# A gated two-branch feed-forward on one core: the median search counts two of its four rows in one packed sum, and all its rounds stand in the second gate/up stage

## The chip, the cores and the metric

The kernel runs on one core of a Trainium2 chip. The metric is the device time of one execution in microseconds (us), the median of several runs. The engines are named as in the profile: PE is TensorE's matmul, PEld its weight load, DVE is VectorE, ACT is ScalarE, POOL is GpSimd, SP is SyncE, which issues every transfer.

## The reference

For 2048 tokens of 1024 features, with an inner width I = 2752:

```
xn = layernorm(x)                               # 2048 x 1024
s  = silu(xn @ w_gate.T)                        # 2048 x 2752
     in each token: the 1376 entries of smallest |s| are set to 0 (ties by index)
s  = (s * (xn @ w_up.T)) @ w_down.T             # branch A
g  = silu((silu(xn @ W_gate.T) * (xn @ W_up.T)) @ W_down.T)   # branch B
out = x + s * g
```

All is in fp32. The kernel keeps that precision by splitting each operand in a high and a low part and making three matmuls for each product (high x high, high x low, low x high).

## The kernel before

The tokens go in four blocks (b = 0 to 3) of 512, four tiles of 128 tokens each. PE goes through four stages in each block:

- **Stage A**: gate and up of branch A. Its results become `keys` (|silu(gate)|, four rows of 2752 fp32 in each partition, one for each token tile) and `prods`.
- **Stage B**, the second gate/up stage: 22 chunks of 128 inner features of branch B (21 whole ones and a half), 48 matmuls of 512 columns for a whole chunk (L875 to L877). After chunk c ACT makes its silu (`silu_b`, L1077), and DVE multiplies it by up (`product_b`, L1554), which frees the chunk's two PSUM banks for chunk c + 4.
- **Stage BD**: the down projection of branch B (L632), from `hid_ring`, which ACT and DVE fill chunk by chunk (`hid_split` and `hid_lo_part`, L1397). Beside it DVE ends the search, corrects ties (`mask_ties`, `mask_prods`) and turns the masked products for branch A (`turn_first`, L1622), whose last transpose releases ACT for `split_turned` and then for the silu of branch B's output (L1136), which PE waits for.
- **Stage AD**: the down projection of branch A (L632 again).

The search for each token's median key needs keys alone. It finds the 31 bits of a float in 31 rounds: a round counts in each of the four rows how many keys lie below a candidate, accepts the bit or not, and posts the next candidate (`cand_ready`). DVE counts rows 0 and 1 (L1380, one instruction a row, a comparison whose results are summed by the accumulator), ACT counts rows 2 and 3 at the same time (`count`, L961). The small instructions behind them (L1384 accept, L1386 bit, L1387 found, L1389 next candidate) are DVE's. Rounds 0 to 29 stand in stage B: two ahead of the first chunk's product, then one or two behind the product of each of the first 20 chunks (`ROUNDS_AFTER`, `TWO_AFTER`). Round 30 stands in stage BD, behind the first four low parts.

In block 0 the weights come raw. ACT makes each tile's high part (`hi`, L928), POOL its low part (`low`, L1206, a subtraction of two tensors in SBUF with 1024 columns; 512 for stage B's last two tiles), and SP writes both to DRAM for the later blocks. In the later blocks stage B's tiles are loaded ready-made, and POOL does nothing in it. In block 0 POOL's low part of each of stage B's tiles 4 to 43 waits until a certain round begins:

```python
c, odd = divmod(m - B0 - 4, 2)
pool.wait_ge(cand_ready, ROUNDS_AFTER[c].start + (odd if c not in BOTH_HIGHS else 0) + 1)
```

A chunk of stage B uses two tiles, the ring holds four, and PE waits for the low part of each tile of block 0.

Of the kernel before, what the change touches and what calls it, by code (L numbers as in the profile page):

```python
# [10 lines left out]
ALU = mybir.AluOpType  # L11
# [5 lines left out]
I = 2752  # L17
K_ZERO = int(0.5 * I)
# [10 lines left out]
NJ = -(-I // P)  # L29
# [44 lines left out]

ROUNDS = 31
DVE_ROWS = 2
ACT_ROWS = NT - DVE_ROWS
PAIRS = 4
GROUPS = NJ // PAIRS
ROUNDS_FIRST = 2  # L80
TWO_AFTER = (1, 4, 6, 9, 11, 14, 16, 19)

ROUNDS_AFTER = []
for chunk in range(PAIRS * GROUPS):
    first = ROUNDS_AFTER[-1].stop if chunk else ROUNDS_FIRST
    ROUNDS_AFTER.append(range(first, first + (2 if chunk in TWO_AFTER else 1)))
ROUNDS_B = ROUNDS_AFTER[-1].stop
# [2 lines left out]
assert all(len(ROUNDS_AFTER[c]) == 1 for c in BOTH_HIGHS)  # L90


LOWS_ROUND = 5
LOWS_CHECK = 7
LOWS_MASKS = ((8, 9, 10, 10, 11, 11), (12, 14, 14, 14, 15, 15), (17, 18, 18, 19, 19, 20), (21, 22, 22, 22, 22, 22))

# [48 lines left out]
assert all(chunk_of(n % 2, n // 4, n // 2 % 2) == K_ORDER[n] for n in range(KC))  # L145
assert TILES % RING == 0 and B0 % RING == 0 and BD0 % RING == 0 and AD0 % RING == 2
assert 2 * TAIL == P and NJ == PAIRS * GROUPS + 2 and NJ == 4 * LOOP4 + 6
assert ROUNDS_B + 1 == ROUNDS and LOWS_MASKS[-1][-1] == NJ

assert AD0 % RING == RING - 2  # L150
assert TURN_FIRST - AHEAD >= -(-16 * NT // SQUARES_STEP)
# [38 lines left out]
def done(b, m):  # L190

    return b * BLOCK + m + 1 + RING
# [55 lines left out]
def build(nc, x, w_a, w_rest, w_b, w_tail, wd_b, wd_a, out):  # L248
# [8 lines left out]
    with ExitStack() as ctx:  # L257
        place = [base]

        def at(name, words_shape, dt, offset):  # L260
            return nc.alloc_sbuf_tensor_at(name, [P, *words_shape], dt, offset=offset)

        def take(nbytes):
            got = place[0]
            place[0] += -(-nbytes // 32) * 32
            assert place[0] <= nc.sbuf_usable_end, place[0]
            return got

        def sem(name):
            return ctx.enter_context(nc.semaphore(name))  # L270
# [6 lines left out]
        keys = key_buf[:, 0:NT * I].rearrange("p (t i) -> p t i", t=NT)  # L277
# [25 lines left out]
        ranks = at("ranks", [I], I16, ranks_at)  # L303
# [15 lines left out]
        def small(name, shape, dt=F32):  # L319
            n = 4  # L320
            for s in shape:
                n *= s
            return at(name, shape, dt, take(n))
# [14 lines left out]
        counts = small("counts", [NT])  # L338
        limits = small("limits", [NT])
        sign_sum = small("sign_sum", [NT])  # L340
        need2 = small("need2", [1])
        found_f = found[:, :].bitcast(F32)
        cand_f = cand[:, :].bitcast(F32)

# [52 lines left out]
        sel_step = sem("sel_step")  # L397
# [524 lines left out]
        def _(act):  # L922
            def hi(b, m):

                if m < TILES and is_split(b, m):
                    q, w = m % RING, width(m)
                    act.wait_ge(landed[q], m // RING * 16 + 16)
                    act.activation(w_hi[q][:, 0:w], w_raw[q][:, 0:w], ACT.Copy).then_inc(hi_ready, 1)  # L928
# [19 lines left out]
            def run(b, first_block):  # L948
                def hid_split(dst, src, rows=P):
                    if rows == TAIL:  # L950

                        act.activation(hid_ring[TAIL:P, dst, 1, :], src[0:TAIL], ACT.Copy)
                    act.activation(hid_ring[0:rows, dst, 0, :], src[0:rows], ACT.Copy).then_inc(hid_hi, 1)  # L953

                def count(n):

                    act.wait_ge(cand_ready, b * (ROUNDS + 1) + n + 1)
                    for t in range(DVE_ROWS, NT):
                        if t > DVE_ROWS:
                            act.wait_ge(act_counted, b * (ROUNDS * ACT_ROWS) + n * ACT_ROWS + (t - DVE_ROWS))  # L960
                        act.activation(signs_row[:, :], keys[:, t, :], ACT.Sign, bias=cand_f[:, t:t + 1], scale=-1.0,  # L961
                                       accum_out=counts[:, t:t + 1]).then_inc(act_counted, 1)
# [141 lines left out]
                def signs_of(t):  # L1104
                    if t < DVE_ROWS:
                        act.wait_ge(cand_ready, b * (ROUNDS + 1) + (ROUNDS + 1))
                    else:
                        act.wait_ge(found_ready, b + 1)

                    act.wait_ge(signs_used, b * NT + (2 if t == NT - 1 else 1))  # L1110
                    act.activation(signs[t], keys[:, t, :], ACT.Sign, bias=found_f[:, t:t + 1], scale=-1.0,
                                   accum_out=sign_sum[:, t:t + 1]).then_inc(signed, 1)

                for j in range(NJ):
                    if j + AHEAD < NJ:
                        if j > 0:
                            act.wait_ge(tiles_done, done(b, BD0 + j - 1))
                        if j == 0:
                            act.wait_ge(b_free, b * NJ + (NJ + PAIRS))
                        hid_split((j + AHEAD) % RING, hid_b[:, j + AHEAD, :], P if j + AHEAD < NJ - 1 else TAIL)  # L1120
                        if j + AHEAD >= STAGED:
                            hi(b, BD0 + j + AHEAD)
                    if j == 0:
                        count(ROUNDS_B)
                    for t in range(NT):
                        if j == SIGNS_AT[t]:
                            signs_of(t)
# [50 lines left out]
            for b in range(NB):  # L1178
                run(b, b == 0)
# [84 lines left out]
        def _(dve):  # L1264
            dve.memset(need2[:, :], 0.0).then_inc(consts, 1)
            dve.memset(ones[:, :], 1)
            dve.memset(eps[:, :], EPS)
            dve.memset(limits[:, 0:DVE_ROWS], K_ZERO - 0.5)
            dve.memset(limits[:, DVE_ROWS:NT], 2 * K_ZERO - I - 0.5).then_inc(consts, 1)
            dve.sem_inc(a_free, NT)  # L1270
            dve.sem_inc(b_free, PAIRS)
# [64 lines left out]
                dve.tensor_tensor(xnT[:, k, 1, tokens], ps[:, X_BANK + i, 0:STAGE * P], xnT[:, k, 0, tokens].bitcast(F32),  # L1336
                                  ALU.subtract).then_inc(xn_ready, 1)

            ROUND_STEPS = DVE_ROWS + 3
            CHECK_STEPS = ACT_ROWS + 2  # L1340

            def xn_low(b, n):
# [28 lines left out]
                    dve.tensor_tensor(lo, raw, high.bitcast(F32), ALU.subtract).then_inc(w_low, 1)  # L1371

            def run(b, last_block):
                def search_round(n):
                    dve.wait_ge(cand_ready, b * (ROUNDS + 1) + n + 1)
                    done = b * (ROUNDS * ROUND_STEPS) + n * ROUND_STEPS
                    for t in range(DVE_ROWS):
                        if t > 0:
                            dve.wait_ge(sel_step, done + t)
                        dve.tensor_scalar(ranks[:, :], keys[:, t, :], cand_f[:, t:t + 1], 0.0, ALU.is_lt, ALU.add,  # L1380
                                          accum_out=counts[:, t:t + 1]).then_inc(sel_step, 1)
                    dve.wait_ge(sel_step, done + DVE_ROWS)
                    dve.wait_ge(act_counted, b * (ROUNDS * ACT_ROWS) + n * ACT_ROWS + ACT_ROWS)
                    dve.tensor_tensor(accept[:, :], counts[:, :], limits[:, :], ALU.is_le).then_inc(sel_step, 1)  # L1384
                    dve.wait_ge(sel_step, done + (DVE_ROWS + 1))
                    dve.tensor_scalar(bit[:, :], bit[:, :], 1, None, ALU.logical_shift_right).then_inc(sel_step, 1)  # L1386
                    dve.copy_predicated(found[:, :], accept[:, :], cand[:, :]).then_inc(sel_step, 1)  # L1387
                    dve.wait_ge(sel_step, done + ROUND_STEPS)
                    dve.tensor_tensor(cand[:, :], found[:, :], bit[:, :], ALU.bitwise_or).then_inc(cand_ready, 1)  # L1389
# [156 lines left out]
                def product_b(c):  # L1546
                    pair = c % PAIRS
                    dve.wait_ge(b_silu, b * NJ + (c + 1))
                    dve.wait_ge(tiles_done, done(b, B0 + 2 * c + 1))
                    chunk = hid_b[:, c, :]  # L1550
                    if c == NJ - 1:
                        dve.tensor_tensor(chunk[0:TAIL], ps[TAIL:P, 2 * pair, :], chunk[0:TAIL], ALU.mult).then_inc(b_free, 1)
                    else:
                        dve.tensor_tensor(chunk, ps[:, 2 * pair + 1, :], chunk, ALU.mult).then_inc(b_free, 1)  # L1554

                for n in range(ROUNDS_FIRST):
                    search_round(n)
                for c, rounds in enumerate(ROUNDS_AFTER):
                    product_b(c)
                    for n in rounds:  # L1560
                        search_round(n)
                product_b(NJ - 2)

                dve.wait_ge(b_free, b * NJ + (NJ - 1 + PAIRS))
# [46 lines left out]
                def lows_to(n):  # L1611
                    for j in range(lows[0], n):
                        hid_lo_part(j % RING, hid_b[:, j, :], b * (2 * NJ) + j, j == NJ - 1)
                    lows[0] = n
# [15 lines left out]
                    return dve.transpose(dst, src)  # L1630

                lows_to(AHEAD + 1)
                search_round(ROUNDS_B)
                lows_to(LOWS_ROUND)
                dve.wait_ge(cand_ready, b * (ROUNDS + 1) + (ROUNDS + 1))
                dve.memset(accept[:, :], 0)
                check_found()
# [92 lines left out]
            for b in range(NB):  # L1730
                run(b, b == NB - 1)

            t = NT - 1
# [47 lines left out]
```

## Time and profile before

| what | value |
|---|---|
| median of 3 runs (lowest to highest) | 2782.26 us (2779.91 to 2783.34) |
| the profiled execution's own time | 2784.59 us |
| its span in the profile | 2782.8 us |
| PE busy | 2753.9 us, 99% of the span |
| DVE busy | 2307.4 us, 83% |
| ACT busy | 1352.7 us, 49% |
| POOL busy | 388.3 us, 14% |
| DMA | 614.28 MB, 221 GB/s |

The kernel's time is PE's matmuls and the few places where PE stands still. A faster DVE or ACT shortens it only where PE waits for them. A slower one lengthens it as soon as the reserve between the engines is used up.

### The profile page before, as it was taken

How to read it: one execution, taken by the hardware profiler on the slowest of the kernel's cores; microseconds unless marked ns; L12 is line 12 of the kernel's file. 1: busy time of each engine (PE TensorE's matmuls, PEld its weight loads, DVE VectorE, ACT ScalarE, POOL GpSimd, SP SyncE). 2: the span in 40 equal slices, each digit the busy share in tenths (PEclk: the TensorE clock that was granted, in tenths of full speed). 3: DMA queues.
4: the chain of work that ended last, by engine and by line, in shares of the span. 5: the costliest groups of instructions: out<-in, count | busy, mean ns of one | idle time of the engine just before them, and what ended most of it. 6: DMA issues, size and time to landing. Idle time of an engine off the chain costs nothing. (4 is left out here: it accounts for less than half of the span.)

```text
span 2782.8 us, 31374 instructions
## 1 busy us (share of the span) xinstructions
PE 2753.9 (99%) x12204; PEld 2281.1 (82%) x12204; DVE 2307.4 (83%) x3002; ACT 1352.7 (49%) x1386; POOL 388.3 (14%) x161
## 2 busy tenths in 40 slices
PE   9999999999999999999999999999999999999999
PEld 7778888878788888888878888888887888888887
DVE  7676999999967698998986678999897767999971
ACT  4234998332444477631144557671115446776110
POOL 5565443044400000000020000000011000000000
PEclk9999999999999999999999999999999999999999
DMA  6898888579766555556656655555666664555564
GB/s 235 308 328 286 293 288 280 211 251 357 255 193 196 181 188 192 189 203 219 249 190 195 192 180 190 195 196 194 240 223 195 193 196 173 195 196 193 189 233 170
DMA packets 135097, 614.28 MB, mean 221 GB/s; under 512 B 12752, under 2 KB 12752, under 8 KB 89168
## 3 DMA queue, kind: packets, MB, share of 16 engines
q1 hardware_dynamic: 134992, 612.94, 63.2%
q8 instruction: 58, 0.95, 0.1%
q14 instruction: 47, 0.39, 0.0%
HBM read 492.31 MB, written 120.59 MB: 220 GB/s over the span
## 5 line engine op out<-in xcount | busy, mean ns | idle before, releaser
L632 PE MATMUL ps<-w_split,hid_ring 128*128 128x512 f32 x4096 | 935.2, 390 | 6.8 <-ACT hid_buf L1136 4.6
L632 PEld LDWEIGHTS ps<-w_split,hid_ring 128*128 128x128 f32 x4096 | 769.4, 188 | 171.5 <-issue 7.9
L1380 DVE TENSOR_SCALAR_CACHE_REDUCE ranks<-key_buf,cand 128x2752 int16<-128x2752 f32 x248 | 762.9, 3076 | 5.8
L961 ACT ACTIVATE signs_row<-key_buf,cand 128x2752 bf16<-128x2752 f32 x248 | 642.6, 2591 | 191.6 <-DVE cand L1389 182.0
L877 PE MATMUL ps<-xnT,w_split 128*128 128x512 f32 x1376 | 535.3, 389 | 0.0
L876 PE MATMUL ps<-xnT,w_split 128*128 128x512 f32 x1376 | 535.3, 389 | 0.0
L875 PE MATMUL ps<-xnT,w_split 128*128 128x512 f32 x1376 | 535.3, 389 | 0.0
L1206 POOL TENSOR_TENSOR w_split<-w_raw,w_split 128x1024 fp32r<-128x1024 f32 (+2 forms) x118 | 290.2, 2467 | 377.3 <-ACT w_split L928 137.0
L875 PEld LDWEIGHTS ps<-xnT,w_split 128*128 128x128 f32 x1376 | 258.3, 188 | 53.7
L876 PEld LDWEIGHTS ps<-xnT,w_split 128*128 128x128 f32 x1376 | 258.3, 188 | 53.6
L877 PEld LDWEIGHTS ps<-xnT,w_split 128*128 128x128 f32 x1376 | 258.3, 188 | 53.3
L928 ACT ACTIVATE w_split<-w_raw 128x1024 fp32r<-128x1024 f32 (+2 forms) x118 | 122.8, 1043 | 252.5 <-DMA w_raw<-w_a 125.9
L847 PE MATMUL ps<-w_split,s_split 128*128 128x512 f32 x936 | 217.0, 389 | 0.0
L938 ACT ACTIVATE w_split<-w_raw 128x1024 fp32r<-128x1024 f32 x144 | 151.1, 1050 | 133.7 <-DMA w_raw<-t_dram 76.9
L1371 DVE TENSOR_TENSOR w_split<-w_raw,w_split 128x1024 fp32r<-128x1024 f32 x144 | 172.0, 1210 | 47.1 <-ACT w_split L938 46.8
L847 PEld LDWEIGHTS ps<-w_split,s_split 128*128 128x128 f32 x936 | 175.7, 188 | 36.4
L1227 POOL TENSOR_TENSOR prods<-prods 128x1024 f32<-128x1024 f32 x3 | 8.7, 2906 | 1297.3 <-DVE prods L1354 1297.3
L953 ACT ACTIVATE hid_ring<-key_buf 128x512 fp32r<-128x512 f32 x88 | 54.3, 630 | 268.3 <-PE ps L632 191.3
L847 PE MATMUL ps<-w_split,xnT 128*128 128x512 f32 x720 | 167.6, 390 | 0.0
L953 ACT ACTIVATE hid_ring<-hid_buf 128x512 fp32r<-128x512 f32 x88 | 55.1, 631 | 226.8 <-PE ps L632 225.1
L847 PEld LDWEIGHTS ps<-w_split,xnT 128*128 128x128 f32 x720 | 135.6, 188 | 28.3
L782 PE MATMUL ps<-w_split,xnT 128*128 128x512 f32 (+1 forms) x368 | 140.5, 382 | 5.8 <-POOL w_split L1206 3.4
(146 smaller groups left out, 2907.0 us busy)
## 6 DMA issues: line engine op xcount, KB each, us to landing
w_split<-split SPq DMA_DIRECT2D x272, 1024.0 KB, 4.8
split<-w_split SPq DMA_DIRECT2D x72, 1024.0 KB, 6.8
w_raw<-w_a SPq DMA_DIRECT2D x100, 512.0 KB, 4.2
w_raw<-t_dram SPq DMA_DIRECT2D x78, 512.0 KB, 3.3
w_raw<-w_b SPq DMA_DIRECT2D x42, 512.0 KB, 4.9
w_extra_raw<-t_dram SPq DMA_DIRECT2D x42, 512.0 KB, 3.6
t_dram<-t_buf SPq DMA_DIRECT2D x20, 1024.0 KB, 8.6
w_extra_raw<-w_a SPq DMA_DIRECT2D x30, 512.0 KB, 3.6
```

Of the source, the lines that this page charges most:

```text
L632: ins = pe.matmul(ps[:, 2 * t + half, :], h, w[:, half * TB:(half + 1) * TB], start=(first and n == 0), stop=last and stop)
L782: pe.matmul(ps[:, bank, 0:wide], hi, w_high[:, cols], start=first, stop=False)
L847: ins = pe.matmul(ps[:, W_BANK[p] + t, :], tokens_of(p, pair, n, part, t), w[:, cols], start=(p in (P4, P1, P6, P5) and pair == 0 and n == ...
L875: pe.matmul(ps[:, bank, :], hi, xnT[:, k, 0, :], start=(first and n == 0), stop=False)
L876: pe.matmul(ps[:, bank, :], hi, xnT[:, k, 1, :], start=False, stop=False)
L877: ins = pe.matmul(ps[:, bank, :], lo, xnT[:, k, 0, :], start=False, stop=(last and k == KC - 1))
L928: act.activation(w_hi[q][:, 0:w], w_raw[q][:, 0:w], ACT.Copy).then_inc(hi_ready, 1)
L938: act.activation(high, raw, ACT.Copy).then_inc(hi_ready, 1)
L961: act.activation(signs_row[:, :], keys[:, t, :], ACT.Sign, bias=cand_f[:, t:t + 1], scale=-1.0, accum_out=counts[:, t:t + 1]).then_inc(act ...
L1206: pool.tensor_tensor(w_lo[q][:, 0:w], w_raw[q][:, 0:w], w_hi[q][:, 0:w].bitcast(F32), ALU.subtract).then_inc(lo_ready, 1)
L1371: dve.tensor_tensor(lo, raw, high.bitcast(F32), ALU.subtract).then_inc(w_low, 1)
L1380: dve.tensor_scalar(ranks[:, :], keys[:, t, :], cand_f[:, t:t + 1], 0.0, ALU.is_lt, ALU.add, accum_out=counts[:, t:t + 1]).then_inc(sel_st ...
```

## The change

DVE's two counts become one packed sum. The first instruction compares row 0 with its candidate and writes 4096 for each key below it (no sum). The second compares row 1 (0 or 1 for each key at or above its candidate), adds the first one's result and sums: 4096 x (count of row 0) + (count of row 1). Two instructions of one column take the sum apart by rounding. The limits of rows 0 and 1 change to fit. A chunk's `product_b` moves from ahead of its first round into that round, behind DVE's counts and ahead of the wait for ACT's. `TWO_AFTER` has nine chunks where it had eight, so all 31 rounds stand in stage B, and stage BD has none. `LOWS_ROUND`, which ordered the low parts around the old round 30, is gone. POOL's waits are unchanged in form and follow the new `ROUNDS_AFTER`.

```diff
+PACK = 4096.0
+PACK_ROUND = 1.5 * 2.0 ** 23 * PACK
-TWO_AFTER = (1, 4, 6, 9, 11, 14, 16, 19)
+TWO_AFTER = (1, 3, 6, 8, 10, 12, 14, 16, 18)
-LOWS_ROUND = 5
@@ ACT, stage BD
-                    if j == 0:
-                        count(ROUNDS_B)
@@ DVE
-            dve.memset(limits[:, 0:DVE_ROWS], K_ZERO - 0.5)
+            dve.memset(limits[:, 0:1], PACK * K_ZERO - 0.5)
+            dve.memset(limits[:, 1:2], K_ZERO - I - 0.5)
@@ a round
-                    for t in range(DVE_ROWS):
-                        if t > 0:
-                            dve.wait_ge(sel_step, done + t)
-                        dve.tensor_scalar(ranks[:, :], keys[:, t, :], cand_f[:, t:t + 1], 0.0, ALU.is_lt, ALU.add,
-                                          accum_out=counts[:, t:t + 1]).then_inc(sel_step, 1)
-                    dve.wait_ge(sel_step, done + DVE_ROWS)
+                    dve.tensor_scalar(ranks[:, :], keys[:, 0, :], cand_f[:, 0:1], PACK, ALU.is_lt, ALU.mult).then_inc(sel_step, 1)
+                    dve.wait_ge(sel_step, done + 1)
+                    dve.scalar_tensor_tensor(out=ranks[:, :], in0=keys[:, 1, :], scalar=cand_f[:, 1:2], in1=ranks[:, :],
+                                             op0=ALU.is_ge, op1=ALU.add, accum_out=counts[:, 0:1]).then_inc(sel_step, 1)
+                    dve.wait_ge(sel_step, done + 2)
+                    dve.tensor_scalar(above[:, :], counts[:, 0:1], float(-(I // 2)), PACK_ROUND, ALU.add, ALU.add).then_inc(sel_step, 1)
+                    dve.wait_ge(sel_step, done + 3)
+                    dve.scalar_tensor_tensor(out=counts[:, 1:2], in0=above[:, :], scalar=PACK_ROUND, in1=counts[:, 0:1],
+                                             op0=ALU.subtract, op1=ALU.subtract).then_inc(sel_step, 1)
+                    if product is not None:
+                        product_b(product)
+                    dve.wait_ge(sel_step, done + 4)
                     dve.wait_ge(act_counted, b * (ROUNDS * ACT_ROWS) + n * ACT_ROWS + ACT_ROWS)
                     dve.tensor_tensor(accept[:, :], counts[:, :], limits[:, :], ALU.is_le).then_inc(sel_step, 1)
@@ stage B
                 for c, rounds in enumerate(ROUNDS_AFTER):
-                    product_b(c)
                     for n in rounds:
-                        search_round(n)
+                        search_round(n, c if n == rounds.start else None)
@@ stage BD
                 lows_to(AHEAD + 1)
-                search_round(ROUNDS_B)
-                lows_to(LOWS_ROUND)
```

## Rows read from the trace of the kernel before

**Rows 1.** Page, part 1: busy time, share of the span, instructions.
```profile
PE 2753.9 (99%) x12204; PEld 2281.1 (82%) x12204; DVE 2307.4 (83%) x3002; ACT 1352.7 (49%) x1386; POOL 388.3 (14%) x161
```
**Rows 2.** PE's waits, whole span: us in total, times, longest.
```profile
PE ps L847 <- DVE xnT L1345: 5.0, 3, 2.1
PE ps L632 <- ACT hid_buf L1136: 4.6, 1, 4.6
```
**Rows 3.** Line L632's matmuls: ns min/median/max, first and last start (us).
```profile
L632 PE MATMUL ps<-w_split,hid_ring x4096: 387/389/764, 489.5 to 2777.8; 128*128 128x512 f32 x196
```
**Rows 4.** Windows, stage B of blocks 0, 1: PE, PEld, DVE, ACT, POOL, clock, DMA.
```profile
256.00:490.00 234.00, 234.00 (x1034) 193.81 (x1033) 218.33 (x272) 211.53 (x187) 98.72 (x42) 1.00 0.84 286
960.00:1181.00 221.00, 221.00 (x977) 183.06 (x976) 203.98 (x253) 164.28 (x137) 0.00 (x0) 1.00 0.53 190
```
**Rows 5.** DVE's timeline, block 0: first count, a round, a product (start, us).
```profile
257.49 3.08 DVE L1380 TENSOR_SCALAR_CACHE_REDUCE ranks<-key_buf,cand 128x2752 int16<-128x2752 f32 x1
...
480.28 0.16 DVE L1384 TENSOR_TENSOR accept<-counts,limits 128x4 uint32<-128x4 f32 x1
...
480.95 3.08 DVE L1380 TENSOR_SCALAR_CACHE_REDUCE ranks<-key_buf,cand 128x2752 int16<-128x2752 f32 x1
...
484.07 3.08 DVE L1380 TENSOR_SCALAR_CACHE_REDUCE ranks<-key_buf,cand 128x2752 int16<-128x2752 f32 x1
...
487.19 0.17 DVE L1384 TENSOR_TENSOR accept<-counts,limits 128x4 uint32<-128x4 f32 x1
...
487.67 0.16 DVE L1389 TENSOR_TENSOR cand<-found,bit 128x4 uint32<-128x4 uint32 x1
487.75 0.69 DVE L1554 TENSOR_TENSOR hid_buf<-ps,hid_buf 128x512 f32<-128x512 f32 x1
```
**Rows 6.** ACT's timeline in the same round.
```profile
480.95 2.59 ACT L961 ACTIVATE signs_row<-key_buf,cand 128x2752 bf16<-128x2752 f32 x1 [3.68 <-DVE cand L1389]
...
486.16 0.19 ACT L961 ACTIVATION_READ_ACCUMULATOR signs_row<-key_buf,cand 128x1 f32 x1
```
**Rows 7.** Groups by line and shape: busy us, mean ns; idle before.
```profile
L1459 DVE TENSOR_SCALAR key_buf<-key_buf 128x512 uint32<-128x512 uint32 x60 | 22.8, 424 | 0.0
L1602 DVE TENSOR_SCALAR ranks<-ranks,need 128x2752 int16<-128x2752 int16 x16 | 15.0, 936 | 0.6
L1590 DVE TENSOR_SCALAR ranks<-signs_row 128x2752 int16<-128x2752 bf16 x8 | 7.0, 870 | 0.0
L1418 DVE TENSOR_SCALAR key_buf<-key_buf 128x192 uint32<-128x192 uint32 x16 | 3.1, 255 | 0.1
```
**Rows 8.** Groups by line: two-input and scan instructions of 2752 columns.
```profile
L1592 DVE TENSOR_TENSOR_SCAN ranks<-ranks 128x2752 int16<-128x2752 int16 x16 | 94.3, 5892 | 0.6
L1607 DVE TENSOR_TENSOR prods<-prods,ranks 128x2752 f32<-128x2752 f32 x16 | 48.4, 3026 | 2.3
```
**Rows 9.** Line L1380, all 248 counts: ns min/median/max.
```profile
L1380 DVE TENSOR_SCALAR_CACHE_REDUCE ranks<-key_buf,cand x248: 3069/3079/3081, 257.5 to 2549.2; 128x2752 int16<-128x2752 f32 x124
```
**Rows 10.** Timelines of POOL and DVE at two places of block 0.
```profile
264.01 2.42 POOL L1206 TENSOR_TENSOR w_split<-w_raw,w_split 128x1024 fp32r<-128x1024 f32 x1 [4.48 <-ACT w_split L928]
...
264.20 2.24 DVE L1389 TENSOR_TENSOR cand<-found,bit 128x4 uint32<-128x4 uint32 x1
...
587.27 5.89 DVE L1592 TENSOR_TENSOR_SCAN ranks<-ranks 128x2752 int16<-128x2752 int16 x1
...
589.10 6.25 POOL L1206 TENSOR_TENSOR w_split<-w_raw,w_split 128x1024 fp32r<-128x1024 f32 x1 [3.20 <-ACT w_split L928]
...
593.07 2.83 DVE L1397 TENSOR_TENSOR hid_ring<-hid_buf,hid_ring 128x512 fp32r<-128x512 f32 x1
```
**Rows 11.** Waits of POOL for candidates, whole span.
```profile
POOL w_split L1206 <- DVE cand L1389: 113.9, 26, 7.2
```
**Rows 12.** Windows, PE alone, behind its 4.6 us wait: busy, clock, DMA.
```profile
613.00:621.00 8.00, 8.00 (x25) 0.70 0.50 193
```

More of the change, by code:

```diff
@@ L76 @@
 DVE_ROWS = 2
+PACK = 4096.0
+PACK_ROUND = 1.5 * 2.0 ** 23 * PACK
+assert I < PACK and I // 2 < PACK / 2 and PACK * (I + 1) < 2 ** 24
 ACT_ROWS = NT - DVE_ROWS
@@ L147 @@
 assert 2 * TAIL == P and NJ == PAIRS * GROUPS + 2 and NJ == 4 * LOOP4 + 6
-assert ROUNDS_B + 1 == ROUNDS and LOWS_MASKS[-1][-1] == NJ
+assert ROUNDS_B == ROUNDS and LOWS_MASKS[-1][-1] == NJ
 assert AD0 % RING == RING - 2
@@ L341, in build @@
         need2 = small("need2", [1])
+        above = small("above", [1])
         found_f = found[:, :].bitcast(F32)
@@ L1337, in x_low @@
                                   ALU.subtract).then_inc(xn_ready, 1)
-            ROUND_STEPS = DVE_ROWS + 3
+            ROUND_STEPS = DVE_ROWS + 5
             CHECK_STEPS = ACT_ROWS + 2
@@ L1373, in run, with search_round @@
             def run(b, last_block):
-                def search_round(n):
+                def search_round(n, product=None):
                     dve.wait_ge(cand_ready, b * (ROUNDS + 1) + n + 1)
                     done = b * (ROUNDS * ROUND_STEPS) + n * ROUND_STEPS
-                    for t in range(DVE_ROWS):
-                        if t > 0:
-                            dve.wait_ge(sel_step, done + t)
-                        dve.tensor_scalar(ranks[:, :], keys[:, t, :], cand_f[:, t:t + 1], 0.0, ALU.is_lt, ALU.add,
-                                          accum_out=counts[:, t:t + 1]).then_inc(sel_step, 1)
-                    dve.wait_ge(sel_step, done + DVE_ROWS)
+                    dve.tensor_scalar(ranks[:, :], keys[:, 0, :], cand_f[:, 0:1], PACK, ALU.is_lt, ALU.mult).then_inc(sel_step, 1)
[10 more added lines that the diff above has]
+                    dve.wait_ge(sel_step, done + 4)
                     dve.wait_ge(act_counted, b * (ROUNDS * ACT_ROWS) + n * ACT_ROWS + ACT_ROWS)
                     dve.tensor_tensor(accept[:, :], counts[:, :], limits[:, :], ALU.is_le).then_inc(sel_step, 1)
-                    dve.wait_ge(sel_step, done + (DVE_ROWS + 1))
+                    dve.wait_ge(sel_step, done + (DVE_ROWS + 3))
                     dve.tensor_scalar(bit[:, :], bit[:, :], 1, None, ALU.logical_shift_right).then_inc(sel_step, 1)
```

## The prediction

> **What bounds the kernel now.** I read the page's busy times first. PE is busy for 99% of the span, DVE for 83%, ACT for half, POOL for 14% [rows 1]. So the time can fall only by what PE stands still, some 29 us in all (2782.8 - 2753.9), and it can rise wherever another engine falls behind PE. Next come PE's waits. Most are a microsecond or two at block borders. One alone is large: 4.6 us for ACT's silu of branch B's output [rows 2]. It stands in block 0, between stages BD and AD. Then the windows of stage B, where the rounds are: PE is busy for all of them, in block 0 as in block 1 [rows 4]. The reader is to see in the same rows that DVE is nearly full there (218 of 234 us, 204 of 221), and that block 0 alone has POOL at work beside it: 42 instructions, 98.7 us.
>
> PE cannot get faster in stage B. All the change can win is the 4.6 us in stage BD, and what it can lose is DVE's reserve in stage B.
>
> **A round, before and after.** Before, count to count on DVE takes 3.12 us (480.95 to 484.07, the accumulator's read included), the second count as much (to 487.19), and accept to next count 0.67 us (480.28 to 480.95): 6.91 us [rows 5]. ACT's two counts take 5.4 us (480.95 to 486.35) [rows 6], so DVE sets the pace.
>
> The first new instruction (compare, times 4096) has no sum. Its nearest rows are one-input instructions without a sum: 4-byte ones take 424 ns at 512 columns and 255 at 192 [rows 7], 0.53 ns for each column more, while the count with a sum takes 3079 ns for 2752 [rows 9], 1.1 each. I take the half rate: 424 + 2240 x 0.53 = 1.61 us, plus 0.07 for the candidate read per partition (936 against 870 ns for two int16 instructions with and without such an operand [rows 7]), so 1.68, and 1.71 with the 0.03 gap. Its upper end is the old count without its read, 3.0 us. The second one reads two tensors in SBUF (keys fp32, ranks int16) and sums. The two-input row with just these kinds takes 3026 ns without a sum [rows 8], the summed one-input row 3079. I take 3.12 to the next start. Its upper end is the scan, which runs at half that pace (5892 ns [rows 8]). The two one-column instructions cost 0.20 us each, like the small ones of the tail (487.67 back to 487.19 has such steps). Sum: 1.71 + 3.12 + 0.40 + 0.67 = 5.90 us, and a product inside a round adds 0.65 (0.69 busy [rows 5]).
>
> Where POOL is still (blocks 1 to 3) ACT is about level: 5.4 + 0.1 + 0.67 = 6.2 us for a round. 31 rounds and 20 products take at most 31 x 6.2 + 20 x 0.65 = 205 us. The old order had 230 us for 30 (257.49 to 487.83). So three blocks get slack in stage B. Round 30 leaves stage BD, 6.9 us less for DVE there, but PE waits for nothing in the BD stages of blocks 1 to 3, so these gain nothing. ACT loses its 5.4 us of counting in stage BD too. No transfer is added or moved.
>
> **Block 0: POOL against DVE.** This decides. Look at the two places of [rows 10]. At 264.01 a low part starts on POOL; DVE's candidate instruction of 4 columns with two SBUF inputs starts at 264.20 and takes 2.24 us instead of 0.16: it ends when POOL does. At 589.10 a low part starts under DVE's scan and takes 6.25 us instead of 2.4: it waits for the scan's end (593.1), and then DVE's next two-input instruction at 593.07 takes 2.83 us instead of 0.69, because POOL slipped in between. So the two take turns, each for a whole instruction. The old counts stand outside this: 248 of them lie between 3069 and 3081 ns [rows 9], though POOL's low parts run beside them, started with them by the wait for `cand_ready` [rows 11]. The old order puts each low part under an instruction that does not mind it. The Trainium skill has this rule in "SBUF — State Buffer", Who interferes with whom: one-input instructions with an accumulator output stay clear of the port pair shared with GpSimd, the 2-port modes and two-input ones contend for it, and the pair is held for the whole instruction. By that rule both new instructions contend; the trace agrees for the two-input kind.
>
> In the new kernel POOL's low part is released at the same moment as before, when a round begins. DVE's compare starts in the same moment (before, a count starts 0.2 us behind the candidate). If POOL comes first, the compare waits; if second, POOL slips in behind the compare and the sum waits. Either way DVE loses what the rows show: 2.24 - 0.16 = 2.08, or 2.83 - 0.69 = 2.14, say 2.1 us for each low part. The 20 chunks have 40 low parts with such a gate, 38 of 1024 columns and 2 of 512, and two more stand at the stage's start: 40 x 2.1 + 2 x 1.0 = 86 us. Where two low parts fall in one round (behind a chunk with a single round), the second waits for the sum and then holds up the small two-input instruction behind it, at the same price. ACT's reserve hides nothing, since a round of 8.0 us is above ACT's 6.2.
>
> Stage B of block 0 on DVE: 31 x 5.90 = 183, 20 x 0.65 = 13, and 86, together 282 us. From 257.5 the last candidate is at 539.5. Stage B's last tile's low part waits for that candidate (its gate is round 31's), so 1.3 us of POOL and the second half of the last chunk's matmuls (12 x 0.227 = 2.7 us; 234 us by 1034 [rows 4]) follow: stage BD begins at 543.5, not at 489.5 [rows 3]. That is **54 us** later. The reserve of the ring is included: it shifts where PE stalls, not the sum, since all rounds and products precede stage BD. With lags of this kind PE stops for some 3 us in each chunk; its granted clock then may fall to its lower level (after the 4.6 us stop the window shows 0.70 of 2.4 GHz [rows 12]), but a chunk at DVE's pace of 14 us (282 by 20; against 48 x 0.227 = 10.9) has room for that, so I add nothing.
>
> **The gain.** In stage BD of block 0 DVE is 6.9 us earlier, the last `turn_first` too, ACT's silu with it, and the 4.6 us wait goes, with the clock it cost: 8 us at 0.70 lose 8 x 0.30 = 2.4 us. That is 7.0 us. What is late next is the block border, at 1 to 2 us, unchanged.
>
> **Sum:** 2784.6 + 54 - 7 = 2831.6 for an execution like the profiled one, which lies 2.3 us above the median: **2829 us**.
>
> **The rivals.** 0.2% (5.6 us) is about what a measurement tells from no change.
>
> *No contention worth the name (ends faster).* One mechanism: DVE's sum does not need what POOL holds, because its second input is int16 or because POOL's wait behind the compare puts it beside something harmless. Then only the gain stands: 2782.3 - 7 = 2775. The stage has some 25 us of room (230 less 205), so it holds up to a price of 0.6 us for each of the 42 low parts. For it: no row shows this instruction beside POOL. Against: even 4 columns of a two-input instruction waited 2.1 us. Chance 0.08, and 0.04 for something in between that ends within 0.2%.
>
> *The sum runs at half rate.* Then it takes 5.9 us as the scan does, a round 8.7, and 31 rounds with products 283 us in every block, 53 more than before; block 0 has 86 more. 4 x 53 + 86 - 7 = +291: 3073 us. The Trainium skill warns of this in "Vector Engine (DVE) Microarchitecture Reference", Points that are easy to get wrong: scalar-tensor-tensor with two non-bf16 SBUF sources halves throughput, as no port is left for the accumulator's readback. No row here shows such an instruction wide; the two-input row without a sum runs whole. Chance 0.07.
>
> *The compare does not run at double rate*, so the packed count saves nothing. A round is 7.2 us (3.0 + 3.12 + 0.4 + 0.67), 31 rounds and products 236 us, 6 too many in each block. It would then also be clear of POOL, as the old count is, and only the second low part of a pair (some 10) meets the sum: 4 x 6 + 4 + 21 - 7 = +42, 2824 us. Against: the 4-byte rows at 0.53 ns a column. Chance 0.05.
>
> **Chances and range.** Contention at its price: 0.76, with 2810 to 2845 as its own range (a low part at 1.6 to 2.4 us, the compare up to 0.1 more, a few us of clock). Faster 0.08 + 0.01, within 0.2% 0.03, slower 0.88. The range 2795 to 2855 holds the likeliest but for its far ends, and the slow compare; it leaves out both the gain alone and the half rate.
>
> **What the profile would show.** Stage B of blocks 1 to 3: PE busy throughout, DVE well under 190 us of 221. Stage B of block 0: PE waits for L1206, some 50 us in total over many places; the wide sum at 3.1 us in blocks 1 to 3 and 5.2 in block 0; POOL's low parts over 2.4 us, 4 with the wait for the compare. The wait of 4.6 us for L1136 is gone. I am wrong if the sum's maximum is its median, if PE's waits in stage B of block 0 are nil, or if the wide sum takes near 6 us in all blocks.

## The result, and the profile after

The changed kernel takes 2835.12 us (median of 4 runs, 2833.63 to 2836.62), the kernel before 2782.26 us beside it: a ratio of 1.019, 95% interval 1.0177 to 1.0203. It is 53 us slower. Two executions of the kernel before, one here (4641.44 us) and one in a later sitting (4632.36 us), ran far slower than all its others and stand in no ratio. The forecast was 2829 us, slower, within 2795 to 2855. The profiled execution took 2834.48 us with a span of 2832.7 us.

PE's waits in the changed kernel (us in total, times, longest), answering to [rows 2]:

```profile
PE ps L879 <- POOL w_split L1208: 32.6, 18, 4.1
...
PE ps L636 <- ACT hid_buf L1138: 4.6, 1, 4.6
```

The first row is new: PE stands in stage B (L879 to L881 now) for POOL's low parts (L1208). The second was to vanish and did not. The windows of stage B, blocks 0 and 1 (PE, PEld, DVE, ACT, POOL, clock, DMA), answer to [rows 4], and PE alone to the stretches of block 0's stage:

```profile
256.00:545.00 289.00, 256.38 (x1044) 204.56 (x1043) 277.53 (x308) 216.65 (x191) 112.06 (x42) 0.95 0.68 239
...
1015.00:1235.00 220.00, 220.00 (x972) 182.19 (x971) 175.58 (x286) 166.56 (x141) 0.00 (x0) 1.00 0.54 191
```

```profile
400.00:500.00 100.00, 88.78 (x355) 0.93 0.67 236
```

In block 1 all is as hoped: PE full, DVE down from 204 to 176 us. In block 0 DVE is full for the whole stage (277.5 of 289) and PE is not. Only 33 us of the 50 that the stage grew by are idle PE. The other 18 are PE at work for longer: it is busy for 251.2 us from 256 to 539.8, where the stage took 233.5 before, with its clock at the lower level for some of the time (0.95 and 0.93 of 2.4 GHz). DVE sets the pace, so this is no extra loss but for the stage's last matmuls, and it makes the waits look smaller than they are. Line L636's matmuls tell where stage BD begins, 539.8 against 489.5 us [rows 3]:

```profile
L636 PE MATMUL ps<-w_split,hid_ring x4096: 387/389/763, 539.8 to 2827.8; 128*128 128x512 f32 x196
```

The two wide instructions and the small sum (groups by line: busy us, mean ns; then their ns min/median/max), answering to [rows 9]:

```profile
L1383 DVE SCALAR_TENSOR_TENSOR ranks<-key_buf,cand,ranks 128x2752 int16<-128x2752 f32 x124 | 402.6, 3247 | 4.4
...
L1381 DVE TENSOR_SCALAR ranks<-key_buf,cand 128x2752 int16<-128x2752 f32 x124 | 268.0, 2162 | 4.4
...
L1388 DVE SCALAR_TENSOR_TENSOR counts<-above,counts 128x1 f32<-128x1 f32 x124 | 23.6, 190 | 4.3
```

```profile
L1381 DVE TENSOR_SCALAR ranks<-key_buf,cand x124: 1652/1654/3909, 255.2 to 2573.6; 128x2752 int16<-128x2752 f32 x124
...
L1383 DVE SCALAR_TENSOR_TENSOR ranks<-key_buf,cand,ranks x124: 3083/3085/5111, 258.7 to 2575.3; 128x2752 int16<-128x2752 f32 x124
...
L1388 DVE SCALAR_TENSOR_TENSOR counts<-above,counts x124: 159/159/2095, 262.1 to 2578.6; 128x1 f32<-128x1 f32 x124
```

The medians are the bare prices: 1654, 3085, 159 ns. The means lie above them, by 0.51, 0.16 and 0.03 us. Times 124 that is 63 + 20 + 4 = 87 us of waiting. The old counts had a minimum and a maximum 12 ns apart. How the waiting looks in two rounds of block 0 (DVE's and POOL's timelines: start, us):

```profile
297.97 3.84 DVE L1381 TENSOR_SCALAR ranks<-key_buf,cand 128x2752 int16<-128x2752 f32 x1
301.84 5.11 DVE L1383 SCALAR_TENSOR_TENSOR ranks<-key_buf,cand,ranks 128x2752 int16<-128x2752 f32 x1
...
308.53 3.90 DVE L1381 TENSOR_SCALAR ranks<-key_buf,cand 128x2752 int16<-128x2752 f32 x1
312.46 3.08 DVE L1383 SCALAR_TENSOR_TENSOR ranks<-key_buf,cand,ranks 128x2752 int16<-128x2752 f32 x1
```

```profile
298.01 6.06 POOL L1208 TENSOR_TENSOR w_split<-w_raw,w_split 128x1024 fp32r<-128x1024 f32 x2 [5.71 <-DVE cand L1399]
308.57 2.40 POOL L1208 TENSOR_TENSOR w_split<-w_raw,w_split 128x1024 fp32r<-128x1024 f32 x1 [4.51 <-DVE cand L1399]
```

At 308.57 one low part runs its plain 2.40 us and the compare takes 3.90 in place of 1.65. At 298.01 two low parts follow each other: the first holds up the compare (2.2 us), the second waits for the compare and then holds up the sum (2.0 us).

### The profile page after: what moved, and what is told of

Its sections match the earlier page's. It is cut to its first block and busy times, and to the rows that moved or that the text cites. A ratio compares the mean times of both kernels' runs of the same rounds, so it can differ in the third digit from the quotient of the medians.

```text
span 2832.7 us, 31499 instructions
## 1 busy us (share of the span) xinstructions
PE 2770.5 (98%) x12204; PEld 2287.1 (81%) x12204; DVE 2251.1 (79%) x3127; ACT 1352.6 (48%) x1386; POOL 398.9 (14%) x161
## 5 line engine op out<-in xcount | busy, mean ns | idle before, releaser
L636 PE MATMUL ps<-w_split,hid_ring 128*128 128x512 f32 x4096 | 935.2, 390 | 7.4 <-ACT hid_buf L1138 4.6
L636 PEld LDWEIGHTS ps<-w_split,hid_ring 128*128 128x128 f32 x4096 | 769.3, 188 | 172.1 <-issue 7.9
L879 PE MATMUL ps<-xnT,w_split 128*128 128x512 f32 x1376 | 543.1, 395 | 32.6 <-POOL w_split L1208 32.6
L881 PE MATMUL ps<-xnT,w_split 128*128 128x512 f32 x1376 | 541.5, 394 | 0.0
L880 PE MATMUL ps<-xnT,w_split 128*128 128x512 f32 x1376 | 541.2, 393 | 0.0
L1383 DVE SCALAR_TENSOR_TENSOR ranks<-key_buf,cand,ranks 128x2752 int16<-128x2752 f32 x124 | 402.6, 3247 | 4.4
L1208 POOL TENSOR_TENSOR w_split<-w_raw,w_split 128x1024 fp32r<-128x1024 f32 (+2 forms) x118 | 300.2, 2551 | 416.8 <-DVE cand L1399 155.1
L879 PEld LDWEIGHTS ps<-xnT,w_split 128*128 128x128 f32 x1376 | 261.8, 190 | 95.0 <-POOL w_split L1208 40.4
L881 PEld LDWEIGHTS ps<-xnT,w_split 128*128 128x128 f32 x1376 | 261.6, 190 | 55.1
L880 PEld LDWEIGHTS ps<-xnT,w_split 128*128 128x128 f32 x1376 | 261.7, 190 | 54.5
L1381 DVE TENSOR_SCALAR ranks<-key_buf,cand 128x2752 int16<-128x2752 f32 x124 | 268.0, 2162 | 4.4
```

The costliest lines, as they stand in the source:

```text
L636: ins = pe.matmul(ps[:, 2 * t + half, :], h, w[:, half * TB:(half + 1) * TB], start=(first and n == 0), stop=last and stop)
L879: pe.matmul(ps[:, bank, :], hi, xnT[:, k, 0, :], start=(first and n == 0), stop=False)
L880: pe.matmul(ps[:, bank, :], hi, xnT[:, k, 1, :], start=False, stop=False)
L881: ins = pe.matmul(ps[:, bank, :], lo, xnT[:, k, 0, :], start=False, stop=(last and k == KC - 1))
L1208: pool.tensor_tensor(w_lo[q][:, 0:w], w_raw[q][:, 0:w], w_hi[q][:, 0:w].bitcast(F32), ALU.subtract).then_inc(lo_ready, 1)
L1381: dve.tensor_scalar(ranks[:, :], keys[:, 0, :], cand_f[:, 0:1], PACK, ALU.is_lt, ALU.mult).then_inc(sel_step, 1)
```

## The experiments

Theory 1 is the prediction's: DVE's new instructions and POOL's low parts take turns. Rival 2 is that the new order costs by itself. Each run's ratio is to the kernel before, with its 95% interval.

**POOL writes and does not read.** This is the changed kernel, but the low-part pass of block 0's stage B is left out of the result, for tiles 4 to 43.

```diff
+                if B0 + 4 <= m < BD0:
+                    pool.memset(w_lo[q][:, 0:w].bitcast(F32), 0.0).then_inc(lo_ready, 1)
+                    return
```

> The changed kernel, but in block 0's stage B the low parts of tiles 4 to 43 are not computed: POOL fills them with zero, at the same moments, and reads nothing (the low-part pass of branch B's gate and up in block 0 is left out of the result; all matmuls, waits and transfers stay). Theory 1 (DVE's new instructions and POOL's low parts take turns, 2.1 us for each of some 42): POOL's instruction gets shorter, near 1 us for a write of 1024 columns by the size of DVE's and ACT's one-tensor instructions, so at most half of the 86 us is left and the wide sum, which only shares the read side, is never longer than 3.1 us. Stage B has 25 us of room: 2783 to 2800 us. Rival 2 (the new order of rounds and of the gates stalls PE, whatever POOL reads): the time stays at 2835.

Measured: 2780.1 us, ratio 0.9993 (0.9983 to 1.0002). The whole loss is gone; the time is 3 us below the expected range, which had kept up to half of the waiting. Rival 2 falls, since order, waits and gates are unchanged in the program. The first two fences are DVE's and POOL's timelines, the third the range of the wide sum:

```profile
350.71 1.65 DVE L1384 TENSOR_SCALAR ranks<-key_buf,cand 128x2752 int16<-128x2752 f32 x1
352.40 3.08 DVE L1386 SCALAR_TENSOR_TENSOR ranks<-key_buf,cand,ranks 128x2752 int16<-128x2752 f32 x1
```

```profile
351.01 2.25 POOL L1209 MEMSET w_split<- 128x1024 f32 x1 [4.47 <-ACT w_split L932]
354.37 0.95 POOL L1209 MEMSET w_split<- 128x1024 f32 x1 [1.11 <-ACT w_split L932]
```

```profile
L1386 DVE SCALAR_TENSOR_TENSOR ranks<-key_buf,cand,ranks x124: 3083/3084/3087, 260.2 to 2524.1; 128x2752 int16<-128x2752 f32 x124
```

The write at 354.37 runs beside the wide sum in 0.95 us and leaves it at 3.08. The one at 351.01 comes 0.3 us behind a compare, and takes 2.25 us: it waits for the compare's end at 352.4, then runs. So the compare excludes even a write that comes behind it, and the sum only excludes an instruction of POOL that reads. The Trainium skill states both ("SBUF — State Buffer", Who interferes with whom); the trace agrees, with these numbers. This run changes more than the read, though. The write is shorter than the low part, and it starts at another moment: all but the last of these writes are released by ACT's high part, most of them 0.3 to 0.8 us behind a compare (351.01 against 350.71), and no longer together with the compare by the candidate. Whether a write that comes first would hold up the compare is not shown. That it is the sharing that costs rests on this run together with those below. The 4.6 us wait is still there in this run, although nothing delays stage B.

**Block 0 as before, blocks 1 to 3 as after.**

```diff
+PACKED = (False, True, True, True)      # by block
+ALL_IN_B = (False, True, True, True)    # 31 rounds in stage B, or 30
```

> Block 0 exactly as in the kernel before (two summed counts, 30 rounds in stage B, the 31st in stage BD), blocks 1 to 3 exactly as in the changed kernel. Theory 1: all of the loss is in block 0, where alone POOL computes in stage B, and blocks 1 to 3 neither lose nor gain: 2783 within 3 us. If the packed form costs something in every block (another cost of the new instructions, or of a lack of time in stage B), three quarters of the loss stay, some 2820. If the time freed in stage BD of blocks 1 to 3 were worth something, it would be below 2779.

Measured: 2782.77 us, ratio 1.0003 (0.9994 to 1.0013). All of the loss is in block 0, and the slack of blocks 1 to 3 is worth nothing that the interval (2 us less to 4 us more) could show. The compare's mean there is its plain price:

```profile
L1403 DVE TENSOR_SCALAR ranks<-key_buf,cand 128x2752 int16<-128x2752 f32 x93 | 153.8, 1653 | 3.3
```

**The move alone**: the changed kernel's order, with the old pair of counts in every round.

```diff
+PACKED = (False, False, False, False)
+ALL_IN_B = (True, True, True, True)
```

> The new order alone: 31 rounds in stage B in all blocks, the new chunks with two rounds, the product inside the round, POOL's gates as in the changed kernel, but each round counts its two rows with the old pair of summed instructions. Theory 1: no contention; 31 x 6.91 + 13 = 227 us on DVE against 230, and 1.3 + 2.7 us in block 0 behind the last candidate for the last tile's low part: 2783 to 2795. Rival 2 (the order is what costs): 2825 or more.

Measured: 2783.27 us, ratio 1.0001 (0.9991 to 1.001). 31 old rounds fit into stage B of every block, without packing; stage BD of block 0 begins at 489.6 us. The kernel never needed faster counts to make the move. And the move wins nothing. DVE's timeline in stage BD shows why:

```profile
499.17 0.68 DVE L1432 TENSOR_TENSOR hid_ring<-hid_buf,hid_ring 128x512 fp32r<-128x512 f32 x1
501.58 0.69 DVE L1432 TENSOR_TENSOR hid_ring<-hid_buf,hid_ring 128x512 fp32r<-128x512 f32 x1 [1.73 <-ACT hid_ring L968]
506.79 0.69 DVE L1432 TENSOR_TENSOR hid_ring<-hid_buf,hid_ring 128x512 fp32r<-128x512 f32 x1 [4.52 <-ACT hid_ring L968]
...
528.55 0.69 DVE L1432 TENSOR_TENSOR hid_ring<-hid_buf,hid_ring 128x512 fp32r<-128x512 f32 x1 [0.52 <-ACT hid_ring L968]
```

DVE waits three times for one of ACT's high parts: 1.73 + 4.52 + 0.52 = 6.8 us. That is the 6.9 us that round 30 left; the low part at 520.54 comes at 520.78 in the kernel before, so DVE is ahead no longer. What ACT waited for ahead of these high parts (its timeline):

```profile
500.93 0.61 ACT L968 ACTIVATE hid_ring<-hid_buf 128x512 fp32r<-128x512 f32 x1
506.12 0.63 ACT L968 ACTIVATE hid_ring<-hid_buf 128x512 fp32r<-128x512 f32 x1 [4.58 <-PE ps L647]
...
527.88 0.63 ACT L968 ACTIVATE hid_ring<-hid_buf 128x512 fp32r<-128x512 f32 x1 [2.23 <-PE ps L647]
```

The second and the third wait for PE to free a slot of `hid_ring`. The first shows no wait for PE: ACT came to it at once from its sums over the signs (L1126). PE's slots come 5.44 us apart here (506.12 to 511.56), so by my estimate that slot was free at 500.7, hardly earlier.

**The packing alone**: the old order, the new counts.

```diff
+PACKED = (True, True, True, True)
+ALL_IN_B = (False, False, False, False)   # and the product ahead of the round
```

> The packed count alone: old order (30 rounds in stage B, the 31st in stage BD, product ahead of the chunk's first round), each round with the new packed pair. Theory 1: 30 x 5.90 + 13 + 86 = 276 us in stage B of block 0, so stage BD begins near 535 and not at 489.5: +46 us, 2829 (2820 to 2840). Rival 2: 2783.

Measured: 2815.9 us, ratio 1.0113 (1.0096 to 1.013). The packing carries the loss, but 34 us of it (27 to 36 by the ratio's interval), not 46 as I expected: the value lies below the expected range. Stage BD begins at 522.0 us, 17.8 before the changed kernel's. Where a product stands ahead of a round (DVE, then POOL):

```profile
486.30 0.69 DVE L1590 TENSOR_TENSOR hid_buf<-ps,hid_buf 128x512 f32<-128x512 f32 x1
486.91 3.37 DVE L1404 TENSOR_SCALAR ranks<-key_buf,cand 128x2752 int16<-128x2752 f32 x1
```

```profile
486.46 2.37 POOL L1221 TENSOR_TENSOR w_split<-w_raw,w_split 128x1024 fp32r<-128x1024 f32 x1 [5.71 <-DVE cand L1425]
```

POOL starts under the product, which has one input in PSUM and takes its usual 0.69 us, so the compare waits 1.7 us and not 2.2. That gave theory 4, on the place of the product, tested last.

**The low parts on DVE.** All the work is done and nothing is shared: DVE computes the low parts of tiles 4 to 43 behind its counts.

```diff
+                    if b == 0:
+                        for m in LOWS_IN[n]:     # the tiles whose gate is this round
+                            dve_low(m)           # waits for hi_ready, one tensor_tensor
```

> The changed kernel, but in block 0's stage B DVE itself computes the low parts of tiles 4 to 43, one or two behind the counts of each round, and POOL is still. The work is all done; only the sharing is gone. Theory 1: each costs DVE its own 1.24 us (the 1210 ns of the later blocks' low parts and a gap) in place of 2.1 us of waiting: 257.5 + 183 + 13 + 50 = 503, so stage BD begins near 505 to 508, and the time is 2798 (2792 to 2806). A theory in which it is the mere number of low parts in DVE's path, or the gates, that costs: no change from 2835, or more.

Measured: 2799.54 us, ratio 1.0064 (1.0049 to 1.008), as theory 1 said. Stage BD begins at 503.0 us, 2 us before the expected 505 to 508. DVE is better off doing POOL's 40 instructions itself, at 1.2 us each, than waiting for them:

```profile
403.45 1.22 DVE L1388 TENSOR_TENSOR w_split<-w_raw,w_split 128x1024 fp32r<-128x1024 f32 x1
```

**The low parts of stage BD later in DVE's order**, on three bases: the move with old counts; old counts in block 0 and packed ones elsewhere, all with 31 rounds in stage B; and the changed kernel.

```diff
-LOWS_CHECK = 7
-LOWS_MASKS = ((8, 9, 10, 10, 11, 11), (12, 14, 14, 14, 15, 15), (17, 18, 18, 19, 19, 20), (21, 22, 22, 22, 22, 22))
+LOWS_CHECK = 5
+LOWS_MASKS = ((6, 8, 8, 9, 9, 10), (11, 12, 13, 13, 13, 14), (15, 16, 17, 17, 18, 18), (20, 21, 21, 22, 22, 22))
```

> The new order with the old counts (as in the run of the move alone), and in stage BD the low parts of branch B's hidden chunks stand later in DVE's order: one after the check in place of three, and one to three fewer ahead of each later step. Theory 3: the 6.9 us that round 30 leaves free in stage BD are spent on waiting for these low parts, which can't be made until PE has freed their ring slots (waits of 1.7, 4.5 and 0.5 us in the run of the move alone). With the waits gone, the last transposes end some 7 us earlier, the 4.6 us wait of PE goes, and with it 2.4 us of lower clock: 2776 (2773 to 2779). Rival: DVE's end in stage BD is set by its turns with POOL, which fall anew and eat the gain: 2781 to 2785.

> As the run before, with packed counts in blocks 1 to 3 and the old counts in block 0. If slack in stage B of blocks 1 to 3 is worth nothing, it equals the run before: 2776 (2773 to 2779). If it is worth something, it is 2 us or more below it.

> The changed kernel with the later low parts in stage BD, nothing else. Theory 3: it gains the 7 us that the prediction had counted: 2828 (2825 to 2831). Stage B of block 0 stays as slow. Rival: 2833 to 2837.

Measured: 2777.11 us, ratio 0.9987 (0.9978 to 0.9996); 2777.8 us, 0.9986 (0.9977 to 0.9995); 2828.84 us, 1.0172 (1.0157 to 1.0188). The first lies 6.2 us below its base (2783.27), the third 6.3 below its own (2835.12). The bases ran in other sittings; by the ratios to the kernel before, taken within a sitting, it is 3.9 and 5.0 us. The second has no base that was run. PE's start of stage AD in the first of them, where 4.6 us stood:

```profile
607.94 7.29 PE L647 MATMUL ps<-w_split,hid_ring 128*128 128x512 f32 x31 [1.83 <-DVE hid_ring L1432]
```

The clock behind it no longer falls (PE alone, against the 0.70 of [rows 12]):

```profile
608.00:616.00 8.00, 8.00 (x36) 1.00 0.99 365
```

So the term of the gain exists, in the changed kernel too, but only once the low parts are moved, and not as it was written: the wait does not go, it shrinks from 4.6 to 1.8 us. In the third run the parts are 4.58 less 1.83 here, 1.55 less 0.17 at PE's wait for a low part of POOL just before, and 2.3 us of lower clock (8 us at 0.71 in the changed kernel, at 1.00 here): 6.4 us, where the spans differ by 6.5. The first two beat the kernel before by a little more than their intervals and are the fastest kernels of this study; packing gives the second nothing over the first.

**The later low parts alone**, on the kernel before (round 30 in stage BD).

```diff
+PACKED = (False, False, False, False)
+ALL_IN_B = (False, False, False, False)   # with the LOWS_CHECK and LOWS_MASKS above
```

> The kernel before with the later low parts in stage BD and nothing else (the 31st round stays in stage BD). Theory 3: both parts are needed. With round 30 in the way DVE waits for hardly any low part in stage BD (1.2 us in all before), so there is nothing to win: 2782 within 2 us. If the order alone gave the gain of the run with the move and the later low parts, it would be 2777.

Measured: 2784.59 us, ratio 1.0009 (1.0 to 1.0018): no gain, and 0.6 us above what was expected. Both the move and the order are needed. DVE had nothing to wait for there, and now PE waits for it (L1432's idle time, and PE's wait):

```profile
L1432 DVE TENSOR_TENSOR hid_ring<-hid_buf,hid_ring 128x512 fp32r<-128x512 f32 x84 | 58.5, 710 | 0.6
```

```profile
PE ps L647 <- DVE hid_ring L1432: 7.4, 3, 2.9
```

**The product ahead of the round**, in the changed kernel.

```diff
+                    if not INSIDE[b]:
+                        product_b(c)
                     for n in rounds:
-                        search_round(n, c if n == rounds.start else None)
+                        search_round(n, c if n == rounds.start and INSIDE[b] else None)
```

> The changed kernel, but with the chunk's product ahead of its first round, as before the change (packed counts, 31 rounds in stage B, the new chunks with two rounds). The run of the packed count alone came out 19 us below the changed kernel, 10 more than its 31st round with a low part (8 us) explains. Theory 4: a product ahead of the round reads PSUM and runs while POOL's low part, released by the same candidate, is already at work, so it hides some 0.5 us of each wait; inside the round it hides nothing. 20 products: 10 us less than the changed kernel, 2825 (2822 to 2829). Rival: the place of the product is worth nothing and it is the last tile's gate that costs: 2833 to 2837.

Measured: 2824.15 us, ratio 1.0151 (1.0136 to 1.0167): 11 us below the changed kernel, as theory 4 said. Its stage BD begins 10.3 us earlier. Of this 1.3 us is an earlier start of the search (253.96 against 255.22), and 8.1 us a shorter way on DVE from the first to the last compare (263.2 us against 271.3):

```profile
L647 PE MATMUL ps<-w_split,hid_ring x4096: 387/389/767, 529.5 to 2815.5; 128*128 128x512 f32 x196
```

## Why the prediction was right, point by point

**The bound.** Right: PE lost time only where it waited, and the one place that changed was stage B of block 0.

**The round.** Compare 1.65 us (1.68 taken), sum 3.085 (3.12 with its gap), so neither the half-rate sum nor the slow compare came about. The Trainium skill's warning ("Vector Engine (DVE) Microarchitecture Reference", Points that are easy to get wrong) that a scalar-tensor-tensor instruction with two non-bf16 SBUF sources runs at half throughput does not hold here: 2752 columns with a sum took 3083 ns at least and 3085 in the median of 124.

**POOL against DVE.** Shown, from four sides: the loss vanishes when POOL does not read, when block 0 keeps the old counts, and when the old counts take the new order; and with DVE making the low parts each costs it 1.22 us. The price was right in sum, 87 us against 86. I had left open who comes first. It is POOL nearly always: in block 0 the compare waits in 29 of the 31 rounds and carries 63 of the 87 us, the sum waits in 10 and carries 20, the small sum in 2 and carries 4.

**The sum in stage B.** 54 us taken, 50.3 measured (539.8 less 489.5). The search started 2.3 us earlier (255.2 against 257.5). From the first compare to the last candidate DVE took 278.8 us and not 282, since a product inside a round costs 0.5 us and not 0.65: from the sum's start to the next compare it is 4.66 us with a product (312.46 to 317.12) and 4.18 without (320.99 to 325.17). Behind the last candidate (534.0) PE took 5.8 us and not 4.0, since its clock had fallen in the 4.1 us stop before (its timeline):

```profile
535.41 0.67 PE L879 MATMUL ps<-xnT,w_split 128*128 128x512 f32 x1 [4.07 <-POOL w_split L1208]
535.87 0.63 PE L880 MATMUL ps<-xnT,w_split 128*128 128x512 f32 x1
536.30 0.63 PE L881 MATMUL ps<-xnT,w_split 128*128 128x512 f32 x1
...
539.39 0.39 PE L880 MATMUL ps<-xnT,w_split 128*128 128x512 f32 x1
539.62 0.39 PE L881 MATMUL ps<-xnT,w_split 128*128 128x512 f32 x1
```

The first of these start 0.43 us apart, the last 0.23, as usual: the lower level, 1.2 GHz, and then the full one. The prediction had added nothing for the clock. That held while DVE set the pace, and not here, where PE was the last to finish.

**The gain of 7 us.** This step failed: "In stage BD of block 0 DVE is 6.9 us earlier, the last `turn_first` too, ACT's silu with it, and the 4.6 us wait goes." DVE was earlier by that much behind the check, but not at the last transposes. Between them stand low parts whose high parts come only at the pace at which PE frees their slots, and DVE's order is fixed, so it waited out the same 6.8 us at three of them. In the changed kernel they are these two and a third of 0.5:

```profile
551.82 0.69 DVE L1407 TENSOR_TENSOR hid_ring<-hid_buf,hid_ring 128x512 fp32r<-128x512 f32 x1 [1.73 <-ACT hid_ring L957]
...
557.03 0.69 DVE L1407 TENSOR_TENSOR hid_ring<-hid_buf,hid_ring 128x512 fp32r<-128x512 f32 x1 [4.52 <-ACT hid_ring L957]
```

I had asked what waits for the last transpose and not what DVE itself would wait for on the way. With the low parts later the size comes back (6.3 us of the 7.0), though the wait still stands at 1.8 us. The forecast lay 6 us low for this reason, and would have lain lower but for the 4 us too many in stage B: the two errors partly cancel, and that is luck.

**The signs that I named.** DVE's 176 us in block 1 and the sum's 3.1 us in blocks 1 to 3 came as said. PE's waits in stage B of block 0 are 32.6 us in 18 places and not some 50, because PE ran slower between them. The sum takes 5.1 us in only 10 rounds of block 0, since the compare had mostly waited in its place, and POOL's single low parts keep their plain 2.4. The 4.6 us wait did not go.

**What I did not price.** The product's move into the round costs some 10 us in block 0, since there it no longer covers the start of POOL's low part. My sum had it right by accident: 2.1 us for every low part is the price with the product inside.

**What stays open.** Why POOL wins when both are released by the same candidate was not tried. Nor is it explained what the later low parts cost on the old order beyond the wait shown, if they cost anything (the interval begins at 1.0). Whether a write of POOL that comes first holds up DVE's compare was not tried.

## What to carry to other kernels

A work item that runs free beside another engine may do so because of the form of the neighbour's instruction; before replacing that form by a faster one, ask which engine was placed beside it. Here 1 us saved on a round cost 2.1 us for each neighbour. Where time is taken out of an engine with a fixed order, look for the next instruction in it that waits for the engine you want to speed up: the gain stops there unless that one is moved as well. And test the parts of a combined change singly: here the move was free without the packing, and only with a third edit worth some 4 us (ratio 0.9987).

## What the runs showed of the hardware

A start in the trace does not tell who holds the way to SBUF: at 308.53 the compare is listed 0.04 us ahead of POOL's instruction, and yet waits for it in full (3.90 us), while POOL's takes its plain 2.40. A write that comes 0.3 us behind a compare waits for it (2.25 us in place of 0.95). An instruction of one column with two SBUF inputs also waits, for up to 2.1 us (L1388's maximum of 2095 ns against 159).
